# When a batch's statistics are summed across the partitions: two sums, one bias and a few small steps of stage 1 at other places in their engines' programs

## The reference

```python
x = x + _L0_conv_ref(_gn(x), Wa, ba, Wb, bb, Wg, bg, Wo, bo)   # a = v@Wa+ba, b = v@Wb+bb, g = sigmoid(v@Wg+bg), (g * (a@b)) @ Wo + bo
x = x + _L1_conv_ref(_gn(x), w_off, b_off, w_def)              # relu, 3x3 conv to offsets, bilinear samples at them, 3x3 conv of the samples

def _gn(v, G=32, eps=1e-05):
    g = v.reshape(B_, G, C_ // G, H_, W_)
    m = jnp.mean(g, axis=(2, 3, 4), keepdims=True)
    s = jnp.var(g, axis=(2, 3, 4), keepdims=True)
    return ((g - m) / jnp.sqrt(s + eps)).reshape(v.shape)
```

## Time and profile before

| what | value |
|---|---|
| median of three runs | 1555.24 us |
| profiled execution | 1554.93 us, span of its instructions 1553.1 us |
| TensorE matmul busy | 1475.3 us, 95% of the span |
| VectorE busy | 1057.3 us, 68% |
| ScalarE busy | 1036.0 us, 67% |
| GpSimd busy | 1006.9 us, 65% |
| stage 1 | from 0 to about 335 us of the span |
| mean granted TensorE clock | 0.980 of full speed |

### The profile page before, as it was taken

How to read it: one execution, slowest core, us unless ns; L and a number is a source line. 1 busy time by engine, 2 the same in 40 slices (tenths; PEclk the granted TensorE clock), 3 DMA queues, 4 the chain that set the end, 5 groups by cost and what they waited for, 6 DMA issues and landing times.

```text
span 1553.1 us, 28171 instructions
## 1 busy us (share of the span) xinstructions
PE 1475.3 (95%) x9363; PEld 987.8 (64%) x9364; DVE 1057.3 (68%) x2155; ACT 1036.0 (67%) x1884; POOL 1006.9 (65%) x627
## 2 busy tenths in 40 slices
PE   4999999964999999999999999999999999999997
PEld 3777777742566666666666666666666666666664
DVE  4988888863666666666666666666666666666664
ACT  2555555535777777777777777777777777777762
POOL 3555555634777667777776677777667777766671
PEclk9999999975999999999999999999999999999999
DMA  4333433334666666666666666666666676666660
GB/s 134 111 113 116 120 112 112 105 123 127 191 196 202 200 196 200 196 198 200 203 193 198 198 200 199 201 193 199 197 192 200 184 211 203 200 191 201 184 175 29
DMA packets 190711, 268.12 MB, mean 173 GB/s; under 512 B 19810, under 2 KB 128382, under 8 KB 190590
## 3 DMA queue, kind: packets, MB, share of 16 engines
q1 hardware_dynamic: 190590, 266.60, 58.8%
HBM read 188.33 MB, written 78.18 MB: 172 GB/s over the span
## 4 chain that ended last, share of the span: by engine, by line
PE 74%; SPq 1%; DMA 1%; POOL 1%; DVE 0%; ACT 0%; issue 0%; POOLq 0%; DVEq 0%
PE bank L854 33%; PE pair L822 24%; PE pair L870 7%; PE pair L899 7%; PE pair L837 2%; POOL weights L1681 1%; DMA hat_x<-hats 0%; SPq L628 0%; DMA hx_all<-hat_x 0%; SPq L611 0%; SPq L617 0%; ACT dist L1073 0%; SPq L632 0%; DVE hats L1377 0%; POOL offs_parts L1692 0%
## 5 line engine op out<-in xcount | busy, mean ns | idle before, releaser
L1681 POOL TENSOR_TENSOR weights<-hy_all,hx_all 112x768 f32<-112x768 f32 x384 | 746.9, 1979 | 324.8 <-PE bank L854 303.3
L1392 DVE SCALAR_TENSOR_TENSOR samples_lo<-bank,samples_hi 128x288 f16<-128x288 f32 (+1 forms) x1024 | 452.5, 462 | 356.9 <-ACT samples_hi L1080 351.3
L854 PE MATMUL bank<-weights,zT 112*128 112x288 f32 (+1 forms) x2176 | 597.0, 403 | 0.3 <-DVE samples_lo L1392 0.3
L1080 ACT ACTIVATE samples_hi<-bank 128x288 f16<-128x288 f32 (+1 forms) x1024 | 393.7, 418 | 205.6 <-PE bank L854 189.0
L854 PEld LDWEIGHTS bank<-weights,zT 112*128 112x128 f32 x2176 | 380.9, 190 | 132.0 <-DVE samples_lo L1392 28.9
L822 PE MATMUL pair<-samples_hi,w_hi 128*128 128x512 f16 x576 | 218.9, 380 | 1.3 <-DVE samples_lo L1392 1.3
L822 PE MATMUL pair<-samples_lo,w_hi 128*128 128x512 f16 x576 | 217.6, 378 | 0.0
L822 PE MATMUL pair<-samples_hi,w_lo 128*128 128x512 f16 x576 | 217.4, 377 | 0.0
L870 PE MATMUL pair<-ident,z 128*112 128x128 f32 x1088 | 172.3, 273 | 3.3 <-DVE zT L1412 2.6
L870 PEld LDWEIGHTS pair<-ident,z 128*112 128x112 f32 x1088 | 133.1, 134 | 59.3 <-DVE zT L1412 3.3
L1588 POOL TENSOR_TENSOR samples_lo<-samples_hi,samples_lo 128x512 f16<-128x512 f32 x64 | 74.2, 1159 | 126.1 <-ACT samples_lo L985 126.0
(11 more groups left out here) (142 smaller groups left out, 1774.1 us busy)
## 6 DMA issues: line engine op xcount, KB each, us to landing
hy_all<-hat_y SPq DMA_DIRECT2D x384, 192.0 KB
hx_all<-hat_x SPq DMA_DIRECT2D x384, 192.0 KB
hat_y<-hats SPq DMA_DIRECT2D x256, 126.0 KB
raw<-x_pad SPq DMA_DIRECT2D x68, 272.0 KB, 4.6
x_pad<-hy_all SPq DMA_DIRECT2D x64, 272.0 KB, 3.4
weights<-in_x SPq DMA_DIRECT2D x64, 256.0 KB, 3.0
out<-y SPq DMA_DIRECT2D x32, 512.0 KB, 3.6
hat_x<-hats SPq DMA_DIRECT2D x128, 72.0 KB
```

The lines of the kernel that those rows point to most:

```text
L854: mm = nc.tensor.matmul(sampled_step(n, p)[:, :, c0 - first:c1 - first], zT[0:WPIX, u * WINDOWS + w, :], weights[0:WPIX, u, :, c0:c1], sta ...
L1080: nc.scalar.activation(samples_hi[:, u, :, c0:c1], sampled_step(n, p), ACT.Copy).then_inc(samples_ready, 1)
L1392: nc.vector.scalar_tensor_tensor(out=samples_lo[:, u, :, c0:c1], in0=sampled_step(n, p), scalar=1.0, in1=samples_hi[:, u, :, c0:c1], op0=A ...
L1681: nc.gpsimd.tensor_tensor(to, hy_all[0:WPIX, i * TROWS:(i + 1) * TROWS, :], hx_all[0:WPIX, i * TROWS:(i + 1) * TROWS, :], ALU.mult).then_i ...
```

## The change

The two sums of a batch move up in TensorE's program, `norm_bias` moves behind `gated` in VectorE's, GpSimd's five bias steps move from groups 0 to 4 to groups 3 to 7, and SyncE's three transfers of the bias from group 7 to group 56.

```diff
-BIAS_STEPS = 8
+BIAS_STEPS, BIAS_SPLITS = 8, 5
...
-                if isinstance(g, int) and g == 7:
+                if isinstance(g, int) and g == GROUPS - XR:
                     sp.wait_ge(bias_set, BIAS_STEPS)
...
                 for b, j in ((B_A, 0), (B_G, 2)):
                     nc.tensor.matmul(bank[b], w_abg_hi[:, j], xT_hi[:], start=True, stop=False)
                     nc.tensor.matmul(bank[b], w_abg_lo[:, j], xT_hi[:], start=False, stop=False)
+                ahead = batch_ahead(g, s)
+                if ahead:
+                    mean_sum(*ahead)
                 if not known or g + 1 < GROUPS:
                     turn(g + 1, (s + 1) % XR)
...
                 mm.then_inc(b_done, 1)
+                if ahead:
+                    var_sum(*ahead)
                 nc.tensor.matmul(bank[B_G], w_abg_hi[:, 2], xT_lo[:], start=False,
                                  stop=True).then_inc(g_done, 1)
-                ahead = batch_ahead(g, s)
-                if ahead:
-                    mean_sum(*ahead)
                 if not known or g > 0:
                     gate(g - 1)
-                if ahead:
-                    var_sum(*ahead)
...
-                if batch:
-                    norm_bias(*batch)
                 dve.wait_ge(ab_done, g + 1)
...
                 nc.vector.tensor_tensor(gated[:], bank[B_AB], gT[:],
                                         ALU.mult).then_inc(gated_ready, 1)
+                if batch:
+                    norm_bias(*batch)
...
-                if isinstance(g, int) and g < 5:
-                    split_bias(g)
+                if isinstance(g, int) and XR - BIAS_SPLITS <= g < XR:
+                    split_bias(g - (XR - BIAS_SPLITS))
```

## The result

The changed kernel takes 1560.64 us (median of 8 runs), the kernel before, run beside it, 1555.24: 5.4 us or 0.35% more by these medians. The ratio estimated from the runs is 1.0039 with a 95% interval of 1.0030 to 1.0048, that is 4.7 to 7.5 us. The profiled execution took 1560.08 us, with a span of 1558.3 (before 1554.93 and 1553.1). The forecast was 1561.5.

The account below looks back on a forecast made before the run. Stage 1 was bound by a loop through TensorE's turn and ScalarE's norm, in batches also GpSimd, the power and `nbias`. 13 batches x 0.44 = 5.7, last 0.9, start 0: +6.6 on 1554.93, 1561.5 us; range 1557.2 to 1564.9.

Parts of the forecast that it names:

- The mean sum waits for the row means, and the turn behind it: TensorE, batch group: sum reached at 0.86, row means done at 1.09, so the turn starts at 133.72, not 133.11.
- The delay D: Lateness of the turn in a batch group: wait 0.05, weight load 0.19, sum 0.14; 0.61 us, bounds 0.40 and 0.78.
- What D does: Chain from turn to next norm: the following group starts 0.44 us later per batch, bounds 0.23 and 0.61, nothing paid back.
- Norm, cast, low part, `x_bo` and power follow the turn without slack: Batch chain behind the turn: each starts when the one ahead is done, so the power ends the turn's full delay later.
- my reading that the `variance` is not on the path: VectorE, batch group before the change: `vare` is written while `x_bo` runs, and the power must await `x_bo` anyway.
- The smaller lag of `nbias`: VectorE behind the power: `nbias` follows by 0.05 instead of 0.22 if VectorE is free, winning 0.17 us a batch.
- `vare` starts inside the low part and ends with it: VectorE beside GpSimd's low part: `vare` starts at 136.5 to 136.7 and ends at 137.55, no longer starting with `x_bo`.
- The rival in which `x_bo` holds it: `vare` held through `x_bo` in every batch, norm 1.32 later: 18.5 us more, 1573.4 us; chance 0.06.
- `norm_bias` behind `gated` costs nothing: VectorE's order in a batch: no cost if `gated` ends before the power; forecast ends 139.56 and 139.91.
- the cover of 0.35: Margin in us by which `gated` was to end ahead of the power; without it `nbias` waits for `gated`.
- The last batch, 0.9: GpSimd's weight work delays `dev`, so variance sum, g's low product, cast and low part come later: 0.9 us, bounds 0.2 and 1.2.
- The bias steps "fall into GpSimd's idle time": GpSimd's steps moved to groups 3 to 7 fit its idle 1.86 us ahead of the low part; no cost counted.

Follow-up runs that it names:

- the first variant: Changed kernel with the mean sum right behind the turn, no longer ahead of it: 1557.38 us, ratio to before 1.0018; run again unchanged, 1557.77 us.

## Why the prediction was right, and where it was not

The forecast of 6.6 more held: 5.4 measured, the 14 pairs 6.0. Its steps:

- **The mean sum waits for the row means, and the turn behind it.** Right, shown from three sides: alone it costs all that the change costs in the loop; put behind the turn, or with its input sooner, the pair is within 0.02 of the kernel before; and with the variance sum out of the way too, its place is worth 0.59 (10.52 to 9.93). The delay D was 0.53 and 0.60 in turn from batch to batch, 0.61 forecast.
- **What D does: "D - 0.17: 0.44 a batch".** Mis-sized; it measured 0.33. "Norm, cast, low part, `x_bo` and power follow the turn without slack" was the step that failed: the power came only 0.44 later for a norm 0.56 later. In the kernel before it waited for `vare`, which lasted to the end of `x_bo`, so my reading that the `variance` is not on the path was wrong by that much; with `vare` done in the low part's time the power follows `x_bo` 0.14 sooner. The smaller lag of `nbias` was forecast with 0.17 and measured 0.18.
- **`vare` starts inside the low part and ends with it.** Right: forecast end 137.55, measured 137.63, low part's end 137.60. The rival in which `x_bo` holds it (18.5 us) did not come.
- **`norm_bias` behind `gated` costs nothing.** Right, but `gated` ended at 139.77 and the power at 139.82: of the cover of 0.35 there was 0.05 left.
- **The last batch, 0.9.** Mis-sized: 1.28, above its bound of 1.2. The path was the forecast one, through `dev`, g's low product, the cast and the low part, which starts 1.27 later (4.81 for 3.54). My own times gave 1.16 for that (306.6 for 305.44), of which I counted 0.9 without a row for the difference; nothing was given back, the second norm is 1.29 late. The late turn has no share in it: with the turn early again the pair is 12.19 too. With the variance sum at its old place the late turn does cost 0.46 (10.91 to 11.37).
- **The bias steps "fall into GpSimd's idle time".** Wrong in one place: the step in group 6 stands right behind the power and holds `nbias` by 0.5. That is a term of 0.45 (11.02 to 10.57 when it is undone) that the sum lacked. No measured time shows a gain at the start (0 forecast); the ninth tile's load took the place of the bias, as foretold (38.09 for 38.5).

By the measured terms, against the first trace of the kernel before, the loop's 12 batches of 0.33 cost 3.95, group 6 0.75 and the last batch 1.28: 5.98. Against its second trace it is 3.75, 1.02 and 1.28: 6.05. What is shown is where these come from. The 0.6 between them and the 5.4 lies within the interval, is less than the scatter of the start and of stage 2 between executions, and stays unassigned.

That the sum of 6.6 came so near is in part luck. The forecast had 13 x 0.11 = 1.4 too much in the batches; the bias step in group 6 that it lacked (0.45) and the last batch (0.4 too little) made up for 0.85 of that. The wait and its place on the path are not luck: the experiments show them.

## What to carry to other kernels

Before moving an instruction forward in an in-order engine's program, compare when its input is ready with when the engine gets there: here the 0.23 us between 0.86 and 1.09 put the chain that sets the group's length behind a side chain. A side chain's work belongs in the first place where it neither waits nor stands ahead of something that another engine waits for; here that was one step later for each of two sums, and turned 5.4 us lost into 3.5 gained. And an operation on one engine can be held by an unrelated one on another: look in the trace for small VectorE operations on the path that end together with a long GpSimd one, and place them elsewhere.

## What the runs showed of the hardware

Three small VectorE operations, `vare`, `dev` and `nbias`, lasted until the GpSimd operation had ended that was running when they started, and GpSimd was not delayed: `vare` took 0.75, 0.90 or 1.31 as its start lay in the low part or at `x_bo`'s start, and 0.17 when it started 0.01 ahead of `x_bo`; `dev` took 1.05 instead of 0.16, `nbias` 0.63 instead of 0.13 to 0.16, while the low part kept its 1.15 to 1.17 and `x_bo` its 1.26 to 1.32. Not every small operation is held. `spread`, the one ahead of `vare`, ran inside the low part of the changed kernel (from 136.44) and took 0.14, and `row_means` took its usual 0.16 or 0.17 beside `x_bo`:

```profile
136.55 0.14 DVE L1130 SCALAR_TENSOR_TENSOR spread<-bank,mg 128x4 f32<-128x4 f32 x1
```

The Trainium skill, Advanced Engine Details and Errata, section Miscellaneous Facts (GPSIMD Details), says that the two engines share a read and a write interface, in conflict where VectorE uses two ports or two inputs from SBUF. `dev` and `nbias` with their two inputs from SBUF agree with it, and so does `spread`, one of whose two inputs is a PSUM bank. `vare` has one input; whether it used two ports no row shows. In every held case GpSimd had started first, or in the same 0.01 us, and VectorE was the one that waited.

TensorE's clock did not fall at the same places in two executions of one kernel. Two stretches from each of two executions of the first variant: the group behind the start and group 60, which has no batch work (core 0: us of the stretch, busy us of TensorE, its weight loads, VectorE, ScalarE and GpSimd, granted clock, DMA share, GB/s). First the one, then the other:

```profile
45.37:50.02 4.65, 4.64 (x43) 3.83 (x41) 4.56 (x9) 2.63 (x4) 2.48 (x5) 1.00 0.40 118
...
313.09:317.37 4.28, 4.28 (x38) 3.61 (x39) 2.23 (x5) 2.64 (x4) 4.28 (x4) 1.00 0.09 28
```

```profile
46.03:51.56 5.53, 5.53 (x41) 4.29 (x40) 4.44 (x9) 2.64 (x4) 2.04 (x5) 0.80 0.33 99
...
314.83:320.54 5.71, 5.71 (x38) 4.29 (x39) 2.21 (x4) 2.70 (x4) 5.50 (x6) 0.73 0.07 21
```

Group 60 took 4.28 at a granted clock of 1.00 and 5.71 at 0.73, its second product 0.38 at the higher level (2.4 GHz) and 0.63 at the lower one (1.2 GHz). TensorE had been idle for 1.8 us shortly before in both, behind the late norm of the last batch. The 1.43 is not all lost, since group 61 took 4.28 in the slower execution and 4.70 in the other. In all group 63 starts 2.75 later in the second execution, 1.77 of which it already had at group 6: as much as the gain of some of these edits, in single traces of one program. The Trainium skill, TensorE: Matmul & The Clock Gate, Part 1, says that the number of products at the low clock varies from run to run of one kernel; these rows agree.
